# One transposed norm with a factor per token, and a down product that waits pair by pair

## The reference

```
z = _layernorm(x, ln1_g, ln1_b)          # x here is xn already
qkv = z @ w_in.T + b_in
q, k, v = jnp.split(qkv, 3, axis=-1)
k = q
scores = jnp.einsum('nhld,nhsd->nhls', q, k) * scale
attn = jax.nn.softmax(scores, axis=-1)
out = jnp.einsum('nhls,nhsd->nhld', attn, v)
...
h = jnp.einsum('bsd,fd->bsf', x, _ternary(W1)) + b1
h = jax.nn.gelu(h, approximate=False)
out = jnp.einsum('bsf,df->bsd', h, _ternary(W2)) + b2
...
xn = _layernorm(x, axis=-1)
x = x + attn(xn, ...) + ffn(xn, ...)
```

## Time and profile before

| | |
|---|---|
| Median of 3 runs | 1458.14 us (1456.97 to 1460.0) |
| Profiled execution, span from first to last instruction | 1462.7 us |
| PE, DVE, ACT, POOL busy | 1396.9, 1351.0, 1243.2, 113.7 us |
| Mean granted TensorE clock | 0.987 |

### The profile page before, as it was taken

How to read it: one execution, slowest core, us unless ns; L and a number is a source line. 1 busy time by engine, 2 the same in 40 slices (tenths; PEclk the granted TensorE clock), 3 DMA queues, 4 the chain that set the end, 5 groups by cost and what they waited for, 6 DMA issues and landing times.

```text
span 1462.7 us, 31753 instructions
## 1 busy us (share of the span) xinstructions
PE 1396.9 (96%) x13166; PEld 445.3 (30%) x13166; DVE 1351.0 (92%) x1430; ACT 1243.2 (85%) x2284; POOL 113.7 (8%) x246
## 2 busy tenths in 40 slices
PE   6899988999999999999999999999999999999999
PEld 4666542222222222222222222222222222222244
DVE  7767789999999999999999999999999999999944
ACT  5564543999999999999999999899999999999975
POOL 2000006000000000000000000000111100001100
PEclk8999998999999999999999999999999999999999
DMA  5012000000000000000000001001212100011122
GB/s 228 15 40 69 30 15 1 28 30 29 29 30 29 30 30 29 26 26 29 29 30 29 30 29 34 30 31 34 59 59 59 59 30 32 31 32 59 38 92 86
DMA packets 28529, 60.65 MB, mean 41 GB/s; under 512 B 6200, under 2 KB 11736, under 8 KB 28130
## 3 DMA queue, kind: packets, MB, share of 16 engines
q1 hardware_dynamic: 27810, 56.99, 11.5%
q10 hardware_dynamic: 576, 1.65, 0.3%
HBM read 41.29 MB, written 16.77 MB: 40 GB/s over the span
## 4 chain that ended last, share of the span: by engine, by line
DVE 54%; PE 37%; ACT 5%; issue 3%; DMA 2%; POOL 0%; SPq 0%; ACTq 0%; DVEq 0%
DVE part_max L838 50%; PE ps L367 13%; PE ps L384 8%; PE ps L330 5%; PE ps L1067 3%; ACT w L1046 3%; PE ps L1136 2%; PE ps L1082 2%; DVE w L830 1%; PE ps L458 1%; ACT w L1017 1%; DMA rows<-in_rows 1%; PE ps L439 1%; PE ps L1108 1%; ACT hidden L1012 1%
## 5 line engine op out<-in xcount | busy, mean ns | idle before, releaser
L838 DVE TENSOR_REDUCE part_max<-ps 128x1 f32<-128x1024 f32 x1024 | 1171.5, 1216 | 16.8 <-PE ps L330 13.8
L1046 ACT ACTIVATE w<-ps 128x512 f32<-128x512 f32 x2048 | 1104.5, 596 | 86.5 <-PE ps L384 50.6
L367 PE MATMUL ps<-w,v_ones 128*32 128x256 f32 (+1 forms) x7440 | 623.8, 407 | 0.4
L384 PE MATMUL ps<-qry,key 50*128 50x512 f16 x1984 | 424.1, 389 | 21.2 <-ACT w L1046 20.7
L330 PE MATMUL ps<-qry,key 48*128 48x512 f16 x2048 | 412.6, 381 | 15.1 <-DVE part_max L838 11.7
L367 PEld LDWEIGHTS ps<-w,v_ones 128*32 128x32 f32 x7440 | 146.6, 108 | 371.1 <-issue 206.8
L384 PEld LDWEIGHTS ps<-qry,key 50*128 50x128 f16 x1984 | 103.9, 93 | 475.3 <-ACT w L1046 443.2
L330 PEld LDWEIGHTS ps<-qry,key 48*128 48x128 f16 x2048 | 102.2, 95 | 46.1 <-DVE part_max L838 33.1
L637 POOL COPY v_ones<-v_all 128x128 f32<-128x128 f32 x64 | 18.6, 291 | 805.8 <-PE ps L367 805.8
L1067 PE MATMUL ps<-w_ternary,w 128*128 128x256 f16 x512 | 62.1, 278 | 6.2 <-DVE w L830 6.2
L1008 ACT ACTIVATE q_split<-ps,sigma_bq 128x512 f16<-128x512 f32 x16 | 11.0, 687 | 66.2 <-PE ps L1082 66.2
(11 more groups left out here) (144 smaller groups left out, 462.4 us busy)
## 6 DMA issues: line engine op xcount, KB each, us to landing
key<-q_parts SPq DMA_DIRECT2D x64, 128.0 KB
qry<-q_parts SPq DMA_DIRECT2D x64, 128.0 KB
o_heads<-o_evacuated SPq DMA_DIRECT2D x31, 256.0 KB, 10.2
resid<-in_x SPq DMA_DIRECT2D x8, 512.0 KB, 13.9
q_parts<-q_split SPq DMA_DIRECT2D x16, 256.0 KB, 2.5
key<-q_parts SPq DMA_DIRECT2D x64, 64.0 KB
qry<-q_parts SPq DMA_DIRECT2D x64, 64.0 KB
out<-resid SPq DMA_DIRECT2D x7, 512.0 KB, 3.6
```

The source lines that it names most:

```text
L367: mm = eng.matmul(pv[32 * c:32 * c + 2 * D, c0:c1], vst[:, kb, :], prob[kb % 2][:, c * BANK + c0:c * BANK + c1], start=(kb == 0), stop=(kb ...
L384: eng.matmul(ring_bank(v, i, False), key[v][r:r + KROWS, kb * P:(kb + 1) * P], qry[v][r:r + KROWS, c * BANK:(c + 1) * BANK], start=True, s ...
L838: dve.tensor_reduce(part_max[:, a // 2, a % 2:a % 2 + 1], pa[a % 2], AX.X, ALU.max).then_inc(s_r, 1)
L1046: act.activation(prob[kb % 2][:, c * BANK:(c + 1) * BANK], ring_bank(k, i, last), ACT.Exp, scale=exp_scale).then_inc(s_e, 1)
```

## The change

Only `xn` is normalised, transposed and split; `zn`, `z1`, `z2`, their transposes and their buffers are gone. The q and v products take `x1` and `x2` as operands. What z differs by, a factor per token, is multiplied in as the results leave PSUM. For v the tokens lie on partitions, and the factor is a column of `f_col`. For q the tokens lie along the free dimension, so the factor must be the same row on all 128 partitions: the columns are stored to DRAM (`store_factors`) and loaded back by a broadcasting DMA into `f_row` (`load_factors`). DVE multiplies q by it into a new buffer `qt`, and both parts of q are made from that. ACT's `x1` now waits for the value products of the group before. The down product waits for the pairs of hidden blocks one by one while it computes tiles 0 and 2 together, then does tiles 1 and 3.

```
-            for src, dst in ((xn, tr_x), (zn, tr_z)):
-                for k in range(KC):
...
+            def store_factors(g):
+                sp.wait_ge(s_fc, 2 * (g + 1))
+                sp.dma_start(f_dram[g].rearrange("(t p) -> p t", p=P), f_col[:, g % 2, :], allow_slow_non_contiguous=True).then_inc(s_fs, 16)
+
+            def load_factors(g):
+                sp.wait_ge(s_fs, 16 * (g + 1))
+                wait(sp, s_qf, KC * g)
+                sp.dma_start(f_row[:, :], f_dram[g:g + 1, :].to_broadcast((P, BANK))).then_inc(s_fl, 16)
...
             def store_q(g):
+                if g + 1 < NG:
+                    load_factors(g + 1)
                 sp.wait_ge(s_q2, KC * (g + 1))
...
+                if g + 2 < NG:
+                    store_factors(g + 2)
...
+                dve.tensor_tensor(f_root[:, :], veps[:, 0, :], rstd[:, 0, :], ALU.mult).then_inc(s_fc, 1)
...
+                dve.scalar_tensor_tensor(out=f_col[:, g % 2, :], in0=f_root[:, :], scalar=1.0 / XS, in1=rstd[:, 1, :],
+                                         op0=ALU.mult, op1=ALU.mult).then_inc(s_fc, 1)
...
+            def q_split(g):
+                dve.wait_ge(s_fl, 16 * (g + 1))
                 for k in range(KC):
...
+                    dve.wait_ge(s_q, KC * g + k + 1)
+                    dve.tensor_tensor(qt[:, k, :], pq[k], f_row[:, :], ALU.mult).then_inc(s_qf, 1)
...
             def group(g, first):
                 act.wait_ge(s_tr, g + 1)
                 wait(act, s_h, KF * g)
+                wait(act, s_v, 2 * g)
                 for k in range(KC):
                     act.activation(x1[:, k, :], tr_x[k], ACT.Copy, scale=XS).then_inc(s_x1, 1)
-                wait(act, s_v, 2 * g)
-                for k in range(KC):
-                    act.activation(z1[:, k, :], tr_z[k], ACT.Copy).then_inc(s_z1, 1)
...
-                    act.wait_ge(s_q, KC * g + k + 1)
-                    act.activation(qp[:, k, 0, :], pq[k], ACT.Identity, bias=sbq_col[:, k:k + 1]).then_inc(s_qa, 1)
+                    act.wait_ge(s_qf, KC * g + k + 1)
+                    act.activation(qp[:, k, 0, :], qt[:, k, :], ACT.Identity, bias=sbq_col[:, k:k + 1]).then_inc(s_qa, 1)
...
+            def ffn_down(g, tiles, between=None):
+                if 0 in tiles:
+                    pe.wait_ge(s_g, KF * (g + 1))
                 for f in range(KF):
...
+                    if 0 in tiles and f % 2 == 0:
+                        pe.wait_ge(s_h2, KF // 2 * g + f // 2 + 1)
+                    for t in tiles:
...
-                    pe.wait_ge(s_h2, KF // 2 * g)
-                    for t in range(TG):
-                        ffn_down(g - 1, t, between_down if t >= TG // 2 else None)
+                    ffn_down(g - 1, (0, 2))
+                    ffn_down(g - 1, (1,), between_down)
+                    ffn_down(g - 1, (3,), between_down)
```

More of the change, by code:

```diff
@@ L148, in attention_ffn @@
         x2 = sb("x2", [P, KC, BANK], F16)
-        z1 = sb("z1", [P, KC, BANK], F16)
-        z2 = sb("z2", [P, KC, BANK], F16)
+        on_k = [sb(f"o_normalised{k}", [P, 2, BANK], F16) for k in range(2)]
         scr = sb("weight_scratch", [P, 4, BANK])
@@ L257, in attention_ffn @@
         s_x2 = sem("x2")
[L258 to L259 removed]
+        s_fc = sem("factor_columns")
+        s_fs = sem("factors_stored")
+        s_fl = sem("factor_rows_loaded")
         s_q = sem("q_psum")
+        s_qf = sem("q_by_factor")
         s_qa = sem("q_part1")
@@ L502, in _ @@
             sp.dma_start(wo[:, :, :].rearrange("p k c -> p (k c)"), w_o).then_inc(s_wo, 16)
-            for g in range(2, NG):
+            def store_factors(g):
[5 more added lines that the diff above has]
+                sp.dma_start(f_row[:, :], f_dram[g:g + 1, :].to_broadcast((P, BANK))).then_inc(s_fl, 16)
+            load_x(2)
+            store_factors(0)
+            load_x(3)
+            load_factors(0)
+            for g in range(4, NG):
                 load_x(g)
@@ L751, in value @@
                 dve.wait_ge(s_v, 2 * g + j + 1)
-                dve.tensor_tensor(v_all[:, g * TG + 2 * j:g * TG + 2 * j + 2, :],
-                                  pq[j].rearrange("p (t c) -> p t c", c=C), bv2[:, :, :], ALU.add).then_inc(s_vd, 1)
+                for t in range(2):
+                    last = dve.scalar_tensor_tensor(out=v_all[:, g * TG + 2 * j + t, :], in0=pq[j][:, t * C:(t + 1) * C],
+                                                    scalar=f_col[:, g % 2, 2 * j + t:2 * j + t + 1], in1=bvs[:, :],
+                                                    op0=ALU.mult, op1=ALU.add)
+                last.then_inc(s_vd, 1)
             def add_ffn(g, j):
@@ L801, in sigma @@
                 dve.wait_ge(s_sg, 8)
-                for j in range(2):
-                    last = dve.tensor_scalar(bv2[:, j, :], bv_sum[:, :], vsc[:, 0:1], None, ALU.mult)
-                last.then_inc(s_sg, 1)
+                dve.tensor_scalar(bvs[:, :], bv_sum[:, :], vsc[:, 0:1], None, ALU.mult).then_inc(s_sg, 1)
             def out_scale():
@@ L1098, in group @@
                 pe.wait_ge(s_ln, 4 * g + 4)
-                wait(pe, s_z, KC * g)
                 wait(pe, s_x2, KC * g)
@@ L1134, in group @@
                     for k in range(KC):
-                        for i, part in enumerate((x1, x2)):
+                        for i, part in enumerate(xp):
                             mm = pe.matmul(pf[f % 2], w1t[:, k, f * P:(f + 1) * P], part[:, k, :],
@@ L1188, in _ @@
             values(NG - 1, 1)
-            pe.wait_ge(s_h2, KF // 2 * NG)
-            for t in range(TG):
-                ffn_down(NG - 1, t, first_a)
+            for tiles in ((0, 2), (1,), (3,)):
+                ffn_down(NG - 1, tiles, first_a)
             pe.wait_ge(s_idh, 1)
```

76 lines of the change are left out of this document (36 added, 40 removed).

## The result

| kernel | median us | lowest to highest | ratio to before [95%] |
|---|---|---|---|
| before | 1458.4 | 1456.97 to 1460.0 | |
| changed | 1479.21 | 1477.93 to 1481.13 | 1.0138 [1.0121, 1.0155] |

The change costs 20.8 us between the medians, where 5.1 were forecast. The profiled execution of the changed kernel took 1481.13 us; its span is 1479.2, 16.5 more than that of the profiled execution before, which lies above its kernel's median.

The account below looks back on a forecast made before the run. Row maxima on DVE are half the chain, but the change acts in the first 240 us, where PE and ACT take turns beside DVE. +7.5 - 1.4 - 0.4 - 0.6 = +5.1 us gives 1463.2, range 1457 to 1468.5.

Parts of the forecast that it names:

- parts 1 and 2: Steady token group: PE's path falls to 20.5 us, DVE's 21.0 decides; each group gains 1.05 us, groups 1 to 3 3.15.
- part 3: Start, group 1: without group 0's z work and with waits by pairs, first gelu at 53.05 us, -3.4 (-2 to -4.5).
- part 4: Sync queue: head DMAs wait behind group 5's factor store; PE stands still about 12.5 us, plus 2.0 of clock loss.
- Head 0 lands 14.7 us later plus 0.5 for the small store.: Sync queue: counted from the first head DMA at 18.45 us after group 3's gelu, head 0 lands at 33.65.
- part 5: Behind the heads: group 5's factor row and group 4's q store land late; group 5's gelu comes 7.5 us later.
- Group 5 to 6: Step between these groups' gelus, with fewer transposes but x1 waiting for the value products: gains 1.4 us (0.8 to 2.0).
- 6 to 7: Step between these groups' gelus: gains 0.4 us, as DVE's six early rows fill it.
- the end: Before the first head: one addition of 0.66 us moves behind head 0's negated maximum, -0.6 us.
- Heads land as soon as they are issued: Rival on head loads: a head takes 8.9 us, the stall is 6.7, sum -1.7, 1456.5 us; chance 0.15.
- The rule of the Trainium skill: 128 KB head loads have outermost dimension 2, so use two of sixteen DMA engines, share 0.13; sum stays +5.1 us.
- The head loads still come before PE needs them: Rival on head loads: no stall, all gains stay, -10.35 us, 1447.8 us; chance 0.07.
- The change gives less than it says: Rival: DVE's wide products or ACT's wait eat the 1.05, the start gives only 2; 1467.7 us; chance 0.08.

Follow-up runs that it names:

- e6: Kernel before with only the pair-by-pair down product, its calls and the new order of row maxima in the last group; 1459.14 us, ratio 0.9983.
- e7: Changed kernel with the old down product, its calls and the old order of row maxima in the last group; 1479.16 us, ratio 1.013.
- e2: Changed kernel in its own queue order, factors stored as 128 pieces of 16 bytes and the row read with a stride by DVE; 1471.55 us, ratio 1.0068.
- e13: Changed kernel in which the sync engine waits for group 4's q store to land before storing group 6's factors; 1470.55 us, ratio 1.0066.
- e14: Changed kernel, 4-byte stores, head 0 loaded ahead of group 5's factor store, which waits until head 0 has landed; 1455.11 us, ratio 0.9956.
- e3: Changed kernel with head 0 loaded before group 5's factor store, heads 1 and 2 after later q stores, and 16-byte factor pieces; 1456.54 us, ratio 0.9976.
- e5: e3 with POOL copying each loaded factor row into token order, so DVE reads it without a stride; 1454.78 us, ratio 0.995.
- e9: e5 with group 0 left out of POOL's copy, so DVE reads that row with the stride; 1453.31 us, ratio 0.9949.

## Why the prediction was wrong

- **Right: the loop (parts 1 and 2).** 21.05 us a group with DVE's path deciding, forecast 21.0. The pairs alone (e6) show that PE's and DVE's paths are level before the change; one norm alone (e7) is 0.36 slower, with PE's longer wait and DVE's for the q product in the loop.
- **Right: the start (part 3).** Forecast 53.05, measured 52.80. The gain is 3.70 where I had 3.4. That it is so close is in part luck: this gelu moves by up to 2.8 us between executions that are alike up to there. The four runs with the changed start have it at 52.1 to 52.9, the six with the old one at 54.3 to 57.2, 3.5 apart in the mean.
- **Right: the mechanism (part 4).** First head DMA 18.25 us after group 3's gelu, forecast 18.45. Its 14.7 us for head 0 with two heads behind it are 15.05 in the trace of the kernel before.
- **The step that failed: "Head 0 lands 14.7 us later plus 0.5 for the small store."** The 0.5 was a guess from issue times, with no row of a store in 4-byte pieces. Head 0 landed 21.5 us after its first DMA; from the 15.05 of the same order without a store that is 6.4 for the store (with 16-byte pieces in the same place, in e2, head 0 took 16.2, so 1.1). So PE waited 18.78 us, not 12.5. The clock fell with it as forecast: 0.50 from 125 to 135 us, 0.68 in the next five.
- **The same term again, in part 5, and larger.** Factor row and q store were to land 41 us after the first head DMA, so that group 5's gelu would come 61.4 us after group 3's. The gelu came 73.64 after it. e13 divides the 12.2 us: 8.5 go when the small store behind the q store is held back, 3.7 stay (160.18 - 95.04 = 65.14 against 61.4), which belongs to the small store ahead of the heads: the q store lands 54.1 us after the first head DMA in the changed kernel, 45.6 in e13, and with 16-byte stores (e2) 41.1, the 41 of the forecast. Part 5 had no term for a store that stands *behind* the one waited for, and I had written that the other factor stores cost nothing.
- **Small misses.** Group 5 to 6 gained 0.77 us (forecast 1.4), 6 to 7 0.63 (0.4), the end lost 1.40 (forecast a gain of 0.6), 2.0 apart; in e13 the same stretch gained 0.5, so that the end was right and the loss goes with TensorE's clock (0.83 against 1.00). Together: 12.0 at group 5, and 0.6, -0.2 and 2.0, make the 14.4 us by which head 0's maximum is later than forecast (19.5 against 5.1). The difference of the medians is 15.7 off. The spans of the two profiled executions differ by 16.5, 3.0 less than at head 0's maximum: what follows it takes 1230.4 us before and 1227.4 in the changed kernel. In the profiles of all sixteen kernels, whose code for the heads is the same, it takes 1226.6 to 1230.4, so this is scatter between executions, with the one before at its upper end. The rest of the 15.7 is between executions too, and I have not divided it.
- **The rivals.** "Heads land as soon as they are issued" is refuted: head 0 takes 15.05 us in the kernel before and 13.5 undisturbed, not 8.9, and the issues of its eight DMAs take only some 5. The rule of the Trainium skill that was weighed there (DMA: Bandwidth & Descriptors, section "Why a DMA increments its semaphore by 16 and not by 1") agrees with e14: with nothing else in flight, from 114 to 118 us, the loads run at a DMA share of 0.13. "The head loads still come before PE needs them" was impossible in this order, but e3, e5 and e9 are that case, and gain 3 to 8 us, not the 10.35 that it was priced at. "The change gives less than it says" is refuted by the start and the steady group.

Not settled: what the chip does with a 4-byte piece. The runs show its latency and what it holds up, not why; no size between 4 and 16 bytes was tried, nor 4-byte pieces that are far apart in DRAM. The Trainium skill, DMA: Bandwidth & Descriptors, section Specifications, says that below 512 bytes a DMA does a read-modify-write and misses line rate. No run here shows a read-modify-write, and 512 bytes is not the line that these runs show: a late landing came with 4 bytes only, while the 16-byte stores ahead of the heads landed within 2.9 us.

## What to carry to other kernels

Where a change adds a transfer in tiny pieces, price it by a row that has such pieces, or keep both ends in the range; then ask what is in flight ahead of it as well as what is queued behind. A queue that waits for a late product must not stand in front of loads that other engines need: order by when things are wanted, and let the late, small store go last. And when two engines' paths are level, try the edits for both together: here each alone gained nothing in the loop (22.06 and 22.42 us against 22.06), and both together 1.0 us.

## What was not expected of the hardware

- A store to DRAM in pieces of 4 bytes landed 7.8 us (128 pieces) to 11.7 us (512) after its issue, one in pieces of 16 bytes after 2.8 and 2.9. While it is under way, transfers behind it and ahead of it on the same queue complete late: head 0 took 21.5 us with it ahead and 15.05 without, in the same order of DMAs; 19.1 with it behind and 13.5 without.
- Two such stores in a row cost as much as one.
- DVE's product of PSUM and an SBUF row read with a stride of 16 bytes took 1064 ns, without a stride 681; POOL's copy of that row mostly took 1.1 us.
